# How the queries are turned in a transformer block on one core: an fp32r product with a cast identity, or an fp32 transposition

## The chip, the cores and the metric

The kernel runs on one core of a Trainium2 chip. The metric is the device time of one execution in microseconds; the median of 3 runs before the change is 634.89 us (634.57 to 635.85).

## The reference

16 sequences of 512 tokens with 256 features pass through an attention block and a linear layer with quantised inputs, each with a layer norm ahead and behind and a residual sum. The attention has 16 heads of 16 features and replaces the exponential by its second-order expansion. What is normalised is the sum of 1 + s + s²/2 over the queries (the kernel can therefore sum products of features over the whole sequence once, instead of forming all 512 x 512 scores).

```python
def _taylor_softmax(x):
    t = 1.0 + x + 0.5 * x * x
    return t / jnp.sum(t, axis=-1, keepdims=True)
h = (x - mu) * jax.lax.rsqrt(var + EPS) * ln_w + ln_b
q = h @ w_q
kv = h @ w_kv
k, v = (kv[..., :DIMS], kv[..., DIMS:])
q, k, v = (to_heads(q), to_heads(k), to_heads(v))
q = _rope(q, theta)
k = _rope(k, theta)
qk = jnp.einsum('bhkd,bhqd->bhkq', q, k) * scale
attn = _taylor_softmax(qk)
wv = jnp.einsum('bhkq,bhqd->bhkd', attn, v)
wv = wv.transpose(0, 2, 1, 3).reshape(B, T, DIMS)
return wv @ w_o
...
x = x + _layernorm(_L0_attn_ref(_layernorm(x, axis=-1), L0_attn_ln_w, L0_attn_ln_b, L0_attn_w_q, L0_attn_w_kv, L0_attn_w_o, L0_attn_theta), axis=-1)
x = x + _layernorm(_L0_ffn_ref(_layernorm(x, axis=-1), L0_ffn_weight, L0_ffn_bias), axis=-1)
```

The linear layer rounds its inputs and its weights in blocks of 32 to a grid of 6-bit values and multiplies them (`xd @ wd.T + bias`).

## The kernel before, in words

The tokens are cut into 64 tiles of 128 (4 to a sequence). Every tile goes through the same stages, and the stages of several tiles are interleaved. The order in which each engine issues its stages is written out in a table: `ORDER` gives, for each engine and stage, the step at which each tile's turn comes, and the function `step` of the engine calls in each step the stages whose turn it is. Engines wait for one another by semaphores only.

The stages of a tile, with the engine on which they run:

- the tile is normalised (VectorE) and turned by TensorE (`turn_z`, L894, two transpositions of 128 x 128); ScalarE copies the upper part (`high_h`, L1241), VectorE the rest (L1613)
- keys and queries (`project_kq`) and values (`project_v`) are products in which the high and the low part of each operand are multiplied in turn (`split_product`, L783, L784, L786)
- VectorE rotates keys and queries; ScalarE rounds the queries to fp32r and writes them as the high part into `qsp` (`high_q`, L1293), and GpSimd the difference as the low part (`low_q`, L1764)
- `turn_q` (L883): TensorE turns `qsp` in four blocks of 128 x 128 into the PSUM bank `ps_tr`, and ScalarE copies the bank to `qT` as fp32r (`copy_q`, L1261)
- products of the key features are summed over the sequence (`sum_features`, L1032, on 32 columns of the array each); once a sequence the sums are turned (`turn_sums`, L1041) and combined (`rest_matrix`, L1050, L1057)
- `select` (L859, five a tile, 512 columns each) sums pairs of query features; ScalarE squares the result (`square`, L1192, L1194); `attend` (L924, L930, on 32 columns each) multiplies by the summed keys
- the attended values go out and in by DMA, are normalised, multiplied by the output weights (`project_out`), rounded, turned (`turn_ffn_input`, L873) and multiplied (`ffn`). In the last two sequences the attended values are turned on the core instead (`turn_quads`, L962, four transpositions, and `turn_attention`, L952).

The bank `ps_tr` is shared by `turn_z`, `turn_q`, `turn_ffn_input` and `project_v`; `turn_bank_is_free` waits for the copies of all that were issued before. A turned block is the product of the block as the array's weights and the identity as what streams through, or a transposition with the same operands. The identity comes by DMA into `small` (`ident`) and is used as it is by all transpositions. For `turn_q` ScalarE casts it once, at the start, to `identr` in fp32r (`cast_identity`, L1102), ahead of the scaled identities of `turn_weights` (L1108 to L1111), for which the first products of the weights wait (`fold_kq`, L796, L799). Before those products TensorE runs 12 pairs of fp32 products of ones (`warm_up`, L825), and two of them at some places of the first steps (`fill`, L825).

Of the kernel before, what the change touches and what calls it, by code (L numbers as in the profile page):

```python
# [7 lines left out]
ACT = mybir.ActivationFunctionType  # L8
AX = mybir.AxisListType
F32 = mybir.dt.float32  # L10
F32R = mybir.dt.float32r
FP8 = mybir.dt.float8e4

P = 128
# [88 lines left out]
        "warm_up": ((0,), (), ()),  # L103
    }),
    "scalar": (71, {
        "cast_identity": ((0,), (), ()),
        "cast_selection": ((2,), (), ()),
        "centre": ((133, 150, 167, 175, 195, 220, 238, 254, 274, 291, 310, 325, 345, 363, 381, 396, 412, 432, 452, 467,
            486, 501, 520, 538, 558, 574, 592, 609, 629, 646, 665, 682, 700, 717, 736, 754, 771, 785, 807, 823, 842,
# [220 lines left out]
            150, 151, 152, 153, 154, 155, 156, 157, 158, 159, 160, 161,)),  # L330
    }),
}
RATE = {"angles": "once", "bias_mean": "once", "cast_identity": "once", "cast_selection": "once", "centre_bias": "once",
    "constant": "sequence", "copy_ffn_weight": "once", "copy_main": "sequence", "copy_rest": "sequence", "copy_sums":
    "sequence", "ffn_weight_mean": "once", "fold_kq": "once", "fold_v": "once", "frequencies": "once", "high_kq":
    "once", "high_v": "once", "invert_denominators": "tail", "invert_sums": "spread", "load_again": "load",
# [11 lines left out]
def places(table, count):  # L348

    first, cycle, last, pitch = table  # L350
    steps = {}
    for index in range(count):
        if index < len(first):
            place = first[index]
        elif index >= count - len(last):
            place = last[index - count + len(last)]
        else:
            place = cycle[index % len(cycle)] + pitch * (index // len(cycle))
        steps[place] = index
    return steps  # L360
# [56 lines left out]
def sandwich(nc, x, w_q, w_kv, w_o, weight, bias, identity, columns, selection, out):  # L417
# [7 lines left out]
    for engine, (pitch, tables) in ORDER.items():  # L425
        for name, table in tables.items():
            plan[name] = places(table + (pitch,), counts[RATE.get(name, "tile")])
            issued[name] = 0
# [10 lines left out]
    def each(n, name, stage, *args):  # L439

        if n in plan[name]:
            stage(Tile(plan[name][n]), *args)
            issued[name] += 1

    def once(n, name, stage):

        if n in plan[name]:
            index = plan[name][n]
            stage(Tile(NT * index + NT - 1))
# [21 lines left out]
    def setup(n, name, stage):  # L471

        if n in plan[name]:
            stage()
# [17 lines left out]
    with ExitStack() as ctx:  # L492
        def sb(name, shape, dt=F32):
            return ctx.enter_context(nc.sbuf_tensor(name, shape, dt))

        def bank(name):
            return ctx.enter_context(nc.psum_tensor(name, [P, 512], F32))

        def sem(name):
            return ctx.enter_context(nc.semaphore(name))  # L500


        ps_tr = bank("ps_tr")
# [8 lines left out]
        ident = small[:, 0:P]  # L512
# [2 lines left out]
        pos = small[:, P + 2:P + 2 + NT]  # L515
        freq_base = small[:, P + 6:P + 14]
        cmat = small[0:NP, P + 32:P + 32 + 2 * HD]
        identr = sb("identr", [P, P], F32R)
        selr = sb("selr", [P, CHUNKS, P], F32R)
        at = P + 32 + 2 * HD  # L520
        th = small[:, at:at + 1]
# [27 lines left out]
        qsp = sb("qsp", [P, 2, NQ, 2, HQ * HD], F32R)  # L549
# [75 lines left out]
        const_in, sel_cast, cols_in, ident_in = sem("const_in"), sem("sel_cast"), sem("cols_in"), sem("ident_in")  # L625
        x0_in, table_chain, angles_done, sines_done, tables_done, ln_scaled = (
            sem("x0_in"), sem("table_chain"), sem("angles_done"), sem("sines_done"), sem("tables_done"), sem("ln_scaled"))
        corner_done, turn_ready, kq_folded, v_folded = sem("corner_done"), sem("turn_ready"), sem("kq_folded"), sem("v_folded")
        wkq_in, wv_in, ffn_in, identr_cast, wo_in = sem("wkq_in"), sem("wv_in"), sem("ffn_in"), sem("identr_cast"), sem("wo_in")
        setup_chain, setup_pool, wd_ready, wdt_done = sem("setup_chain"), sem("setup_pool"), sem("wd_ready"), sem("wdt_done")  # L630
        wdt_copied, floor_set, wdt_centred, wo_centred = sem("wdt_copied"), sem("floor_set"), sem("wdt_centred"), sem("wo_centred")
        wkq_high, wkq_low, wv_high, wv_low, wdt_high, wdt_low, wo_high, wo_low = (
# [144 lines left out]
        def _(pe):  # L777
# [84 lines left out]
            def turn_bank_is_free():  # L862

                wait(pe, hT_low, issued["turn_z"])
                wait(pe, qT_copied, issued["turn_q"])
                wait(pe, xdT_low, issued["turn_ffn_input"])
                wait(pe, v_copied, issued["project_v"])
# [6 lines left out]
                mm.then_inc(xdT_done, 1)  # L874

            def turn_q(t):
                if t.n == 1:
                    pe.wait_ge(identr_cast, 1)
                pe.wait_ge(qlo_ready, t.n)
                turn_bank_is_free()  # L880
                for qd in range(NQ):

                    mm = pe.matmul(ps_tr[:, qd * P:(qd + 1) * P], qsp[:, t.two, qd].rearrange("p a b -> p (a b)"), identr[:, :],  # L883
                                   start=True, stop=True)
                mm.then_inc(qT_done, 1)

            def turn_z(t):
# [174 lines left out]
            def step(n):  # L1062
                idle(n, "fill", fill)
                idle(n, "drain", drain)
                setup(n, "warm_up", warm_up)
                setup(n, "fold_kq", fold_kq)
                setup(n, "fold_v", fold_v)
                each(n, "sum_features", sum_features)
                each(n, "select_2", select, 2)
                each(n, "project_v", project_v)  # L1070
                each(n, "select_3", select, 3)
                each(n, "ffn", ffn)
                each(n, "select_4", select, 4)
                each(n, "turn_q", turn_q)
                once(n, "turn_sums", turn_sums)
                tail(n, "turn_quads", turn_quads)
                each(n, "project_kq", project_kq)
                each(n, "turn_z", turn_z)
                each(n, "select_0", select, 0)
                setup(n, "turn_ffn_weight", turn_ffn_weight)  # L1080
                each(n, "project_out", project_out)
                each(n, "select_1", select, 1)
                each(n, "turn_ffn_input", turn_ffn_input)
                once(n, "rest_matrix", rest_matrix)
                tail(n, "turn_attention", turn_attention)
                each(n, "attend", attend)
# [5 lines left out]
        def _(act):  # L1092
# [3 lines left out]
            act.dma_start(wkqv[:, :, 2 * D:3 * D], kv[:, :, D:2 * D]).then_inc(wv_in, 16)  # L1096
            act.wait_ge(setup_pool, 16)
            act.activation(warm[:], mhalf[:], ACT.Sin)

            def cast_identity():  # L1100
                act.wait_ge(ident_in, 16)
                act.activation(identr[:], ident, ACT.Copy).then_inc(identr_cast, 1)  # L1102

            def turn_weights():

# [223 lines left out]
            def step(n):  # L1329
                setup(n, "turn_weights", turn_weights)  # L1330
                setup(n, "high_v", high_v)
                setup(n, "high_kq", high_kq)
                each(n, "high_q", high_q)
                each(n, "square_4", square, 4)
                each(n, "copy_q", copy_q)
                setup(n, "split_ffn_weight", split_ffn_weight)
                each(n, "square_k", square_k)
                setup(n, "weight_distance_sizes", weight_distance_sizes)
                setup(n, "copy_ffn_weight", copy_ffn_weight)
                each(n, "centre", centre)  # L1340
                once(n, "copy_main", copy_main)
                setup(n, "weight_low", weight_low)
                setup(n, "sum_wo", sum_wo)
                each(n, "square_s", square_s)
                each(n, "square_y", square_y)
                each(n, "high_ffn_input", high_ffn_input)
                setup(n, "centre_bias", centre_bias)
                each(n, "high_h", high_h)
                setup(n, "weight_size", weight_size)
                setup(n, "sum_bias", sum_bias)  # L1350
                each(n, "high_attention", high_attention)
                once(n, "copy_rest", copy_rest)
                each(n, "square_0", square, 0)
                setup(n, "weight_high", weight_high)
                each(n, "square_f", square_f)
                each(n, "square_1", square, 1)
                each(n, "copy_quad", copy_quad)
                once(n, "copy_sums", copy_sums)
                each(n, "square_2", square, 2)
                each(n, "copy_v", copy_v)  # L1360
                setup(n, "cast_identity", cast_identity)
                setup(n, "cast_selection", cast_selection)
                setup(n, "split_wo", split_wo)
                setup(n, "sines", sines)
                each(n, "square_3", square, 3)

            every_step("scalar", step)


# [487 lines left out]
```

## Time and profile before

| | |
|---|---|
| median of 3 runs | 634.89 us |
| the profiled execution | 634.73 us |
| its span, first to last instruction | 632.9 us |
| mean granted TensorE clock | 0.992 |
| TensorE (PE) busy | 607.2 us |
| VectorE (DVE) busy | 579.3 us |
| ScalarE (ACT) busy | 534.0 us |
| GpSimd (POOL) busy | 393.8 us |

All times are microseconds from the first instruction of one profiled execution. Matmuls overlap: the next begins before the last has ended, so that busy times and durations of single matmuls cannot be added; starts can be compared. A row of the timeline that ends in x4 is four instructions of one line, and its second number runs from the first start to the last end. PEld is the load of the weights into the array, which may run ahead while an earlier matmul streams. An L number is a line of the kernel.

### The profile page before, as it was taken

To read this page: it belongs to the slowest core of one execution; us is meant where nothing else is said; L and a number is where in the kernel's file an instruction comes from. 1 tells how busy PE (TensorE), PEld (TensorE's weight loads), DVE (VectorE), ACT (ScalarE), POOL (GpSimd) and SP (SyncE) were. 2 spreads that over 40 slices of the span, in tenths; PEclk is the share of its full clock that TensorE was granted. 3 is DMA by queue.
4 is the path that set the end of the run, shared out by engine and by line. 5 is a ranking of instruction groups with operands and counts; after the bars stand their busy time and mean duration, and the time that the engine had idled before them with its cause. 6 is when DMAs were issued, how large, how long until landed. Compare 5 with 4: busy or idle time off the path is not lost.

```text
span 632.9 us, 22530 instructions
## 1 busy us (share of the span) xinstructions
PE 607.2 (96%) x7588; PEld 470.3 (74%) x7588; DVE 579.3 (92%) x1425; ACT 534.0 (84%) x1505; POOL 393.8 (62%) x597
## 2 busy tenths in 40 slices
PE   8799999999999999999999999999999999999984
PEld 8677667777777787777777777777778777778763
DVE  5999999999999999999999999999999999987796
ACT  4357769898898989989899889899898888899983
POOL 2575366676666567766766777675765767653343
PEclk9999999999999999999999999999999999999996
DMA  7101131222232232223232231323233222230201
GB/s 251 35 3 39 24 76 23 66 77 74 60 95 63 76 91 64 76 49 93 73 105 62 79 83 42 108 55 97 62 83 84 68 49 52 69 85 20 68 27 51
DMA packets 55951, 43.64 MB, mean 69 GB/s; under 512 B 7200, under 2 KB 55712, under 8 KB 55840
## 3 DMA queue, kind: packets, MB, share of 16 engines
q1 hardware_dynamic: 55024, 41.42, 24.6%
q8 instruction: 64, 1.05, 0.7%
q10 hardware_dynamic: 816, 0.79, 0.4%
q14 instruction: 47, 0.39, 0.2%
HBM read 18.65 MB, written 8.39 MB: 43 GB/s over the span
## 4 chain that ended last, share of the span: by engine, by line
PE 87%; ACT 5%; issue 4%; DVE 3%; POOL 1%; POOLq 0%; ACTq 0%; DVEq 0%
PE ps_f L859 12%; PE ps_mt L1032 12%; PE ps_o L930 5%; PE ps_o L924 5%; PE ps_qk L783 5%; PE ps_qk L784 5%; PE ps_qk L786 5%; PE ps_w L783 4%; PE ps_tr L883 4%; PE ps_f L924 4%; PE ps_w L786 4%; PE ps_w L784 4%; PE ps_tr L783 3%; PE ps_tr L873 3%; PE ps_tr L786 2%
## 5 line engine op out<-in xcount | busy, mean ns | idle before, releaser
L1192 ACT ACTIVATE feat<-ps_f 128x512 f32<-128x512 f32 x256 | 147.5, 600 | 13.0 <-PE ps_f L859 12.4
L678 DVE TENSOR_TENSOR kf<-kf 128x672 f32<-128x672 f32 (+1 forms) x128 | 130.4, 1023 | 1.0
L859 PE MATMUL ps_f<-qT,selr 128*128 128x512 f32 x320 | 120.4, 426 | 2.0 <-ACT feat L1192 1.2
L1032 PE MATMUL ps_mt<-kf,vp 128*32 128x153 f32 x2048 | 79.6, 296 | 1.5 <-DVE kf L678 0.5
L1787 POOL TENSOR_TENSOR rs_f<-var_f,mhalf 128x1 f32<-128x1 f32 x64 | 47.9, 749 | 47.5 <-ACT squares_f L1326 46.5
L1787 POOL TENSOR_TENSOR rs_y<-var_y,mhalf 128x1 f32<-128x1 f32 x64 | 47.3, 740 | 41.9 <-ACT squares_y L1304 41.4
L1032 PEld LDWEIGHTS ps_mt<-kf,vp 128*32 128x32 f32 x2048 | 60.3, 109 | 16.7 <-issue 14.5
L1776 POOL TENSOR_TENSOR kf<-kf 128x128 f32<-128x128 f32 x64 | 36.6, 571 | 47.2 <-DVE kf L1543 47.2
L859 PEld LDWEIGHTS ps_f<-qT,selr 128*128 128x128 f32 x320 | 55.2, 188 | 13.3 <-ACT feat L1192 5.4
L1783 POOL TENSOR_TENSOR attT_l<-att,attT_h 128x256 fp32r<-128x256 f32 x56 | 45.0, 805 | 31.1 <-ACT attT_h L1233 31.0
L678 POOL TENSOR_TENSOR kf<-kf 128x224 f32<-128x224 f32 x64 | 58.2, 909 | 3.9 <-DVE kf L1548 3.8
L1764 POOL TENSOR_TENSOR qsp<-kf,qsp 128x256 fp32r<-128x256 f32 x64 | 54.2, 847 | 5.9 <-ACT qsp L1293 5.7
L1787 POOL TENSOR_TENSOR rs_s<-var_s,mhalf 128x1 f32<-128x1 f32 x64 | 43.2, 674 | 20.8 <-ACT squares_s L1319 20.3
L783 PE MATMUL ps_qk<-wkqv_h,hT_l 128*128 128x512 f32 x128 | 54.1, 422 | 0.0
L784 PE MATMUL ps_qk<-wkqv_l,hT_h 128*128 128x512 f32 x128 | 50.7, 396 | 0.0
L1261 ACT ACTIVATE qT<-ps_tr 128x512 fp32r<-128x512 f32 x64 | 38.5, 601 | 10.8 <-PE ps_tr L883 9.7
L1787 POOL TENSOR_TENSOR rs_x<-vx,mhalf 128x1 f32<-128x1 f32 x64 | 43.3, 677 | 4.0
L1194 ACT ACTIVATE feat<-ps_f,small 128x512 f32<-128x512 f32 x64 | 44.3, 693 | 1.6 <-PE ps_f L859 1.4
L924 PE MATMUL ps_o<-feat,main 120*32 120x256 f32 (+1 forms) x576 | 42.0, 361 | 2.4 <-ACT feat L1192 2.0
L1529 DVE TENSOR_TENSOR kf<-ps_qk,cosT 128x512 f32<-128x512 f32 x64 | 43.2, 676 | 1.0 <-PE ps_qk L786 0.6
L930 PE MATMUL ps_f<-feat,rm 64*32 64x256 f32 (+1 forms) x576 | 42.0, 363 | 0.0
L930 PE MATMUL ps_o<-feat,rm 64*32 64x256 f32 (+1 forms) x576 | 42.0, 363 | 0.0
(205 smaller groups left out, 1900.3 us busy)
## 6 DMA issues: line engine op xcount, KB each, us to landing
xc<-L_attn_x SPq DMA_DIRECT2D x16, 512.0 KB, 4.0
result<-fin SPq DMA_DIRECT2D x64, 128.0 KB, 1.9
xa<-L_attn_x SPq DMA_DIRECT2D x15, 512.0 KB, 4.0
heads_out<-osb SPq DMA_DIRECT2D x224, 32.0 KB, 2.0
shares<-sums SPq DMA_DIRECT2D x112, 64.0 KB
sums<-osb SPq DMA_DIRECT2D x224, 2.0 KB
wkqv<-L_attn_w_kv ACTq DMA_DIRECT2D x2, 256.0 KB, 4.6
xa<-L_attn_x SPq DMA_DIRECT2D x1, 384.0 KB, 6.1
```

Source lines behind the costliest of these rows:

```text
L678: return eng.tensor_tensor(dims(row, F_MAIN, [[FW, heads], [HD, NR - 1], [1, HD]]), dims(row, F_LIN, [[FW, heads], [0, NR - 1], [1, HD]]), ...
L783: pe.matmul(out_, xl(c), wh(c), start=c == 0, stop=False)
L784: pe.matmul(out_, xh(c), wl(c), start=False, stop=False)
L786: mm = pe.matmul(out_, xh(c), wh(c), start=False, stop=c == CH - 1)
L859: pe.matmul(ps_f[i % 2][:, :], selr[:, i], queries, start=True, stop=True).then_inc(sel_done, 1)
L924: pe.matmul(attend_bank(e)[VW * j:VW * (j + 1), part(p)], main[0:NP, par, p + 2 * e, VW * j:VW * (j + 1)], feat[0:NP, p2, 2 * e + j % 2, t ...
L930: mm = pe.matmul(attend_bank(e)[VW * j:VW * (j + 1), part(p)], rm[rows, par, p, j], feat[rows, p2, HQ, tokens(p, j)], start=False, stop=Tr ...
L1032: mm = pe.matmul(ps_mt[qd // 2][VW * h:VW * (h + 1), (qd % 2) * NF:(qd % 2 + 1) * NF], vp[:, s2, qd * HQ + h], kf[:, s2, qd * HQ + h, 0:NF ...
L1192: act.activation(feat[:, p2, i], ps_f[i % 2][:, :], ACT.Square).then_inc(squared, 1)
L1764: pool.tensor_tensor(dims(qsp[:, p2], HQ * HD, [[2 * HQ * HD, NQ], [HD, HQ], [1, HD]]), dims(kf[:, p2, 0, 0:1], F_Q, [[HQ * FW, NQ], [FW, ...
L1783: pool.tensor_tensor(attT_l[:, t.two].rearrange("p c n -> p (c n)"), att[:, t.two], attT_h[:, t.two].rearrange("p c n -> p (c n)").bitcast ...
L1787: pool.tensor_tensor(rs[c][:, t.two:t.two + 1], variance[:, t.two:t.two + 1], mhalf[:], ALU.pow).then_inc(rstd[c], 1)
```

## The change

`turn_q` turns the four blocks by a transposition in fp32, with the plain identity, in place of a product in fp32r with the cast identity. The cast, its buffer of 512 bytes a partition and its semaphore go. The lines behind the places where something went move up by some lines.

```diff
-        "cast_identity": ((0,), (), ()),
...
-        identr = sb("identr", [P, P], F32R)
...
             def turn_q(t):
-                if t.n == 1:
-                    pe.wait_ge(identr_cast, 1)
                 pe.wait_ge(qlo_ready, t.n)
                 turn_bank_is_free()
                 for qd in range(NQ):
 
-                    mm = pe.matmul(ps_tr[:, qd * P:(qd + 1) * P], qsp[:, t.two, qd].rearrange("p a b -> p (a b)"), identr[:, :],
-                                   start=True, stop=True)
+                    mm = pe.transpose(ps_tr[:, qd * P:(qd + 1) * P], qsp[:, t.two, qd].rearrange("p a b -> p (a b)").bitcast(F32), ident)
                 mm.then_inc(qT_done, 1)
...
-            def cast_identity():
-                act.wait_ge(ident_in, 16)
-                act.activation(identr[:], ident, ACT.Copy).then_inc(identr_cast, 1)
```

Apart from the cast no instruction goes, comes or moves. On ScalarE the start of its order of instructions was this (warm is a one-column activation that loads the table, wa and wb hold the scaled identities):

```order
4 L1098 ACT_TABLE_LOAD
5 L1098 ACTIVATE warm<-mhalf 128x1
6 L1102 ACTIVATE identr<-small 128x128
7 L1108 ACTIVATE wa<-small,lnwx 128x128
8 L1109 ACTIVATE wa<-small,lnwn 128x128
9 L1111 ACTIVATE wa<-wb,lnwx 128x127
```

and is now this:

```order
4 L1093 ACT_TABLE_LOAD
5 L1093 ACTIVATE warm<-mhalf 128x1
6 L1099 ACTIVATE wa<-small,lnwx 128x128
7 L1100 ACTIVATE wa<-small,lnwn 128x128
8 L1102 ACTIVATE wa<-wb,lnwx 128x127
```

The cast has gone, and what stood behind it moved up by one place. On TensorE this is one place of the body before (a turned tile of queries, L883, between the end of a split product and two selects):

```order
748 L786 MATMUL ps_w<-wdt_h,xdT_h 128x256 x2
749 L883 MATMUL ps_tr<-identr,qsp 128x128 x4
750 L859 MATMUL ps_f<-qT,selr 128x512 x2
751 L1041 MATMUL ps_mt<-small,mts 120x128 x4
752 L894 MATMUL ps_tr<-small,z 128x128 x2
753 L783 MATMUL ps_w<-wo_h,attT_l 128x256
```

and now:

```order
748 L784 MATMUL ps_w<-wdt_h,xdT_h 128x256 x2
749 L879 MATMUL ps_tr<-small,qsp 128x128 x4
750 L857 MATMUL ps_f<-qT,selr 128x512 x2
751 L1036 MATMUL ps_mt<-small,mts 120x128 x4
752 L889 MATMUL ps_tr<-small,z 128x128 x2
753 L781 MATMUL ps_w<-wo_h,attT_l 128x256
```

Nothing moved; the four blocks read `small`, which holds the plain identity, in place of `identr`.

## Rows read from the trace of the kernel before

**Rows 1.** The page: busy shares, clock in tenths by slice, chain by engine.
```profile
PE 607.2 (96%) x7588; PEld 470.3 (74%) x7588; DVE 579.3 (92%) x1425; ACT 534.0 (84%) x1505; POOL 393.8 (62%) x597
...
PEclk9999999999999999999999999999999999999996
...
PE 87%; ACT 5%; issue 4%; DVE 3%; POOL 1%; POOLq 0%; ACTq 0%; DVEq 0%
```

**Rows 2.** Stretches: length, busy us of PE, PEld, DVE, ACT, POOL; clock, DMA, GB/s.
```profile
20.00:40.00 20.00, 18.38 (x190) 15.59 (x189) 19.46 (x40) 7.13 (x19) 12.50 (x17) 1.00 0.10 29
200.00:300.00 100.00, 99.61 (x1277) 77.47 (x1279) 95.58 (x236) 90.69 (x258) 67.40 (x99) 1.00 0.28 71
616.00:633.00 17.00, 7.77 (x43) 6.16 (x41) 11.18 (x32) 6.46 (x25) 6.06 (x10) 0.71 0.14 47
```

**Rows 3.** Groups by line: busy us, mean ns of one, idle before.
```profile
L883 PE MATMUL ps_tr<-identr,qsp 128*128 128x128 f32 x256 | 37.3, 268 | 1.4 <-POOL qsp L1764 1.0
...
L962 PE MATMUL ps_mt<-small,osb 128*128 128x128 f32 x32 | 4.7, 274 | 0.0
...
L883 PEld LDWEIGHTS ps_tr<-identr,qsp 128*128 128x128 f32 x256 | 35.6, 190 | 7.9 <-issue 5.2
...
L962 PEld LDWEIGHTS ps_mt<-small,osb 128*128 128x128 f32 x32 | 3.6, 140 | 0.4 <-issue 0.4
```

**Rows 4.** Timeline of PE, products loaded ahead: start, us, line, operation.
```profile
378.01 0.56 PE L883 MATMUL ps_tr<-identr,qsp 128*128 128x128 f32 x4
378.41 0.68 PE L859 MATMUL ps_f<-qT,selr 128*128 128x512 f32 x2
378.93 0.28 PE L783 MATMUL ps_w<-wo_h,attT_l 128*128 128x256 f32 x1
```

**Rows 5.** Timeline of PE, transpositions loaded ahead, the same neighbours.
```profile
597.27 0.60 PE L962 MATMUL ps_mt<-small,osb 128*128 128x128 f32 x4
597.63 0.72 PE L859 MATMUL ps_f<-qT,selr 128*128 128x512 f32 x2
598.18 0.28 PE L783 MATMUL ps_w<-wo_h,attT_l 128*128 128x256 f32 x1
```

**Rows 6.** Timeline of PE, products not loaded ahead.
```profile
341.39 0.63 PE L883 MATMUL ps_tr<-identr,qsp 128*128 128x128 f32 x4
...
342.38 0.28 PE L783 MATMUL ps_w<-wo_h,attT_l 128*128 128x256 f32 x1
```

**Rows 7.** Timeline of PE, transpositions not loaded ahead.
```profile
593.67 0.63 PE L962 MATMUL ps_mt<-small,osb 128*128 128x128 f32 x4
594.05 0.48 PE L859 MATMUL ps_f<-qT,selr 128*128 128x512 f32 x1
594.37 0.38 PE L873 MATMUL ps_tr<-small,xd 128*128 128x128 f32 x2
```

**Rows 8.** Timeline of PE, products before narrow matmuls.
```profile
314.35 0.56 PE L883 MATMUL ps_tr<-identr,qsp 128*128 128x128 f32 x4
314.83 0.60 PE L1032 MATMUL ps_mt<-kf,vp 128*32 128x153 f32 x12
```

**Rows 9.** Timeline of PE, two transpositions before narrow matmuls.
```profile
173.21 0.38 PE L894 MATMUL ps_tr<-small,z 128*128 128x128 f32 x2
173.51 0.58 PE L1032 MATMUL ps_mt<-kf,vp 128*32 128x153 f32 x9
```

**Rows 10.** Timeline of the start: the cast, and the first product of the weights.
```profile
5.60 0.31 ACT L1102 ACTIVATE identr<-small 128x128 fp32r<-128x128 f32 x1 [1.84 <-DMA small<-identity]
...
10.86 1.03 PE L796 MATMUL ps_f<-wkqv,wa 128*128 128x256 f32 x4
```

**Rows 11.** Waits: who for whom, us in total, times, longest.
```profile
ACT qT L1261 <- PE ps_tr L883: 9.7, 18, 1.7
```

**Rows 12.** Timeline of PE, a pair of fp32 products of ones.
```profile
17.54 0.61 PE L825 MATMUL ps_o<-one 128*128 128x128 f32 x4
```

More of the change, by code:

```diff
@@ L332 @@
 }
-RATE = {"angles": "once", "bias_mean": "once", "cast_identity": "once", "cast_selection": "once", "centre_bias": "once",
+RATE = {"angles": "once", "bias_mean": "once", "cast_selection": "once", "centre_bias": "once",
     "constant": "sequence", "copy_ffn_weight": "once", "copy_main": "sequence", "copy_rest": "sequence", "copy_sums":
@@ L628, in sandwich @@
         corner_done, turn_ready, kq_folded, v_folded = sem("corner_done"), sem("turn_ready"), sem("kq_folded"), sem("v_folded")
-        wkq_in, wv_in, ffn_in, identr_cast, wo_in = sem("wkq_in"), sem("wv_in"), sem("ffn_in"), sem("identr_cast"), sem("wo_in")
+        wkq_in, wv_in, ffn_in, wo_in = sem("wkq_in"), sem("wv_in"), sem("ffn_in"), sem("wo_in")
         setup_chain, setup_pool, wd_ready, wdt_done = sem("setup_chain"), sem("setup_pool"), sem("wd_ready"), sem("wdt_done")
@@ L1360, in step @@
                 each(n, "copy_v", copy_v)
-                setup(n, "cast_identity", cast_identity)
                 setup(n, "cast_selection", cast_selection)
```

## The prediction

> **What bounds the kernel now.** I read the page first: the busy shares, the slices, the shares of the chain that ended last. TensorE (PE) is busy 96% of the span and holds 87% of the chain; its granted clock is full in every slice but the last [rows 1]. Then the stretches: from 200 to 300 us PE is busy 99.61 of 100 us, VectorE 95.58, ScalarE 90.69 [rows 2]. So PE's order of work sets the pace of the body. VectorE has only 4 us in 100 to spare, so a gain on PE need not come through whole. A busy share does not price a matmul, because neighbouring ones overlap: one of 128 columns is shown with 268 ns [rows 3], yet four of them in a row take 0.56 us, not 1.07. The price is therefore read from start to start: when the group starts and when the instruction behind it can start, taken far enough behind it that the pace is regular again.
>
> **The change part by part.** 64 times (once a tile) PE turns four 128 x 128 blocks of queries. Before, each is a product in fp32r with a cast identity (L883, 256 in all); after, a transposition in fp32 with the plain identity. Nothing is moved. The same operation on the same shape stands in this trace: the four transpositions of L962 in the tail, and pairs at L873 and L894. So no price has to be guessed; only the surroundings differ.
>
> The two are slow in different places. The weight load of an fp32r block takes 190 ns, that of a transposition 140 [rows 3]. The row of four products is 0.56 us from first start to last end, and the next matmul starts 0.40 us after the first [rows 4]; the row of four transpositions is 0.60 us, with the next 0.36 us after the first [rows 5]. One matmul of either takes about 0.27 us to its end (268 and 274 ns, rows 3), so the transpositions start (0.60 - 0.27) / 3 = 0.11 us apart. Four kinds of place come out of this.
>
> 1. Weights loaded ahead, a full-width matmul behind (either a select, L859, or a split product). Products: from the group's start, over two selects, to the L783 behind them, 378.93 - 378.01 = 0.92 us [rows 4]. Transpositions with the very same neighbours: 598.18 - 597.27 = 0.91 us [rows 5]. The transpositions let the next matmul start earlier, but that one then holds the engine longer. Gain 0.01 us.
>
> 2. Weights not loaded ahead (the group's first load had to wait), full-width matmul behind. Products: 342.38 - 341.39 = 0.99 us over two selects [rows 6]. Transpositions: 594.37 - 593.67 = 0.70 us over one select [rows 7]; a second one adds 0.23 us, since two selects hold the engine 598.18 - 597.63 = 0.55 us behind transpositions [rows 5] and one holds it 594.37 - 594.05 = 0.32 us [rows 7]; so 0.93. Gain 0.06 us.
>
> 3. Weights loaded ahead, narrow matmuls behind, each on 32 columns of the array (L1032, L924, L1050). Products: 314.83 - 314.35 = 0.48 us until the first narrow one starts [rows 8]. Transpositions: a pair takes 173.51 - 173.21 = 0.30 us [rows 9], two more add 0.22, so 0.52. Loss 0.04 us.
>
> 4. Other transpositions or fill products behind, and the cold places before narrow matmuls: nothing, within 0.02 us each.
>
> How many of each? A group loaded ahead lasts 0.56 us [rows 4] and one that is not 0.63 [rows 6]; the whole line is 37.3 us [rows 3]. From 0.56 n + 0.63 (64 - n) = 37.3 follows n = 43 loaded ahead and 21 not. Going through PE's order of instructions, 9 of the 64 are followed by narrow matmuls, 5 by transpositions or fill, 50 by full-width ones; seven of the nine are of the kind loaded ahead. I take 34 places of the first kind, 17 of the second, 7 of the third, 6 of the fourth.
>
> Sum on PE: -34 x 0.01 - 17 x 0.06 + 7 x 0.04 = -0.34 - 1.02 + 0.28 = -1.1 us.
>
> The cast of the identity (L1102, 0.31 us on ScalarE at 5.60 us) goes, and the scaled identities behind it move up by about that [rows 10]. Their first reader, L796, starts at 10.86 us, after the warm-up products; the cast is covered by some 4 us, so I count nothing. Without that cover it would be 0.3 us. SBUF loses a tile of 512 bytes a partition and everything behind it moves; no row prices that, I take nothing.
>
> A second effect has the other sign. ScalarE copies the turned queries (L1261), and it waits for L883 18 times, 9.7 us in total [rows 11]. In the 43 places loaded ahead the last of four ends at 0.60 instead of 0.56 us. Where ScalarE already waits, that is at most 18 x 0.04 = 0.7 us later. ScalarE has 5% of the chain [rows 1], so nearly all of this lies beside PE's other work; I put down 0.04 us and keep the 0.7 for the range.
>
> Not all of PE's 1.1 us arrives. 17 of the places that gain are those at which PE waited for the split of the queries, and a group that comes up sooner there waits longer. I take the middle of nothing and all weighted by the chain's PE share, about two thirds: -0.7 us. The profiled execution took 634.73 us (span 632.9 and 1.8 around it), so 634.0; it lies 0.16 below the median 634.89, on whose footing this is 634.2 us. A difference under 0.2%, 1.3 us, is what a measurement of this kernel can hardly tell from none.
>
> A rule that speaks against the change: the granted clock is 1.00 from 200 to 300 us with four transpositions a tile already in it, and fell to a mean of 0.71 only after 616 us, where PE is busy 7.77 of 17 us [rows 2]; the transposed groups raise the transpositions from four to eight a tile. The Trainium skill ("TensorE: Matmul & The Clock Gate", Part 4) says that a transposition does not count as activity the way a product does. By that rule eight a tile could let the clock fall; the trace so far shows no sign of it. The sum would stay -0.7 us without it; with it, it is the third rival.
>
> **The rivals.**
>
> Faster than forecast: the gain of kind 2 holds nearly everywhere, because what I called loaded ahead is in the changed kernel limited by loads, and those get shorter. PE's weight loads shrink by 256 x 50 ns = 12.8 us [rows 3]. Price 55 x 0.06 = 3.3 us less 0.3 for the narrow neighbours: 3.0, so 631.9. For it: the fp32r loads, 190 ns, are what spaces the products. Against it: the pair of rows 4 and 5 with equal neighbours shows 0.01.
>
> Slower: the later end decides. The copy of the queries starts 0.04 us later at each of 43 places; it holds up ScalarE's queue (square, copy_v and so on stand behind it, in order), those free PE's banks, and PE waits. Price 43 x 0.04 = 1.7 us, with none of the gain coming through and the narrow places losing 0.3: 636.9. It decides once ScalarE rather than PE is waited for in most tiles; it is at 90.69 of 100 us. Against it: the chain has ScalarE at 5%.
>
> Slower by the clock: in 20 to 40 us, while the pipeline fills, PE is busy 18.38 of 20 us, less densely than later, and there the first turned tiles pass [rows 2]. If the clock fell from its upper to its lower level (2.4 to 1.2 GHz) for 8 us of work, that work would take up to 8 us more. VectorE, busy 19.46 of 20 us there, hides a part; price 3 to 6 us, 639.
>
> That it does not do what it says: the blocks go through as true fp32 products. The fill products of L825 are such; two of them are four records of which each starts about (0.61 - 0.27) / 3 = 0.11 us after the last [rows 12], 0.22 a product. 256 x (0.22 - 0.11) = 28 us more, 662. The existing transpositions each leave one record, so I hold it for very unlikely.
>
> **How the numbers follow.** Forecast 634.2 us, chance 0.68; its own range is 633.0 to 635.8 (all of PE's gain and half as much again; none of it and the whole 0.7 of the copies, plus the spread of the median). Faster rival 0.14; slower by the copies 0.14; by the clock 0.03; not as it says 0.01. The range for 8 in 10 reaches into both near rivals: 632.4 to 636.8. Faster by over 0.2%, below 633.6: 0.08 of the forecast's 0.68 and the 0.14, so 0.22. Slower, above 636.2: 0.02 of the forecast and 0.18, so 0.20. Within: 0.58.
>
> **What would show it.** In the profile after: the four of the query line spaced 0.11 us, a group 0.60 us loaded ahead and 0.63 not, the line's busy sum 64 x 0.6 = 39 us instead of 37.3; their loads 140 ns, PE's load row lower by about 13 us; the matmul behind starting 0.36 us after the group's start; 0.91 us over two selects. ScalarE without the cast and the same start of L796. A clock under 1.00 in any stretch before 616 us would mean the clock rival; more waiting of ScalarE for the turned queries, and of PE for the squares, the copy rival; two records a block the last. The forecast is wrong if the span moves by over 1.3 us with all of these as said: then the waits between engines, not PE's own pace, carried the change.

## The result: no gain, slower by 0.27% in one comparison and not to be told from before in two

In the first comparison (20 runs of each) the changed kernel took 636.13 us in the median, the one before 634.19: ratio 1.0027, 95% interval 1.0017 to 1.0036. The forecast was 634.2 and a gain of 0.7 us; the direction is wrong. Two more comparisons of the same kernel (12 runs against 35 each) gave 0.9999 (0.9981 to 1.0016) and 1.0002 (0.9990 to 1.0015), and the kernel before against itself gave 0.9989 (0.9974 to 1.0005). The first interval overlaps neither of the two others of the changed kernel, so there is a part that the intervals do not cover. What the changed kernel costs lies by the three ratios between 0 and 0.3%; the gain of 0.7 us that was forecast shows in none of them.

The profiled execution after has a span of 634.3 us (before: 632.9). The page, answering to [rows 1]:

```profile
PE 607.2 (96%) x7588; PEld 465.4 (73%) x7588; DVE 580.3 (91%) x1425; ACT 533.4 (84%) x1504; POOL 393.8 (62%) x597
...
PEclk9999999999999999999999999999999999999997
...
PE 87%; ACT 5%; issue 4%; DVE 3%; POOL 1%; POOLq 0%; ACTq 0%; DVEq 0%
```

PE's sum is the same to the tenth, ScalarE has one instruction fewer, the shares of the chain are unchanged, and the clock row reads 9 in every slice but the last (by stretches it is 1.00 up to 616 us). From 200 to 300 us (columns as in rows 2):

```profile
200.00:300.00 100.00, 99.65 (x1281) 76.67 (x1284) 95.49 (x236) 90.38 (x259) 67.58 (x99) 1.00 0.27 71
```

The groups by line, answering to [rows 3] (L879 is the old L883):

```profile
L879 PE MATMUL ps_tr<-small,qsp 128*128 128x128 f32 x256 | 39.0, 275 | 1.2 <-issue 0.9
...
L879 PEld LDWEIGHTS ps_tr<-small,qsp 128*128 128x128 f32 x256 | 29.6, 140 | 8.9 <-issue 5.3
```

39.0 us and 140 ns are the forecast values; a transposition leaves one record, so it is one. The row of the loads is lower by 6.0 us (35.6 to 29.6), the sum of PEld by 4.9, where 12.8 was forecast: 256 x 50 ns counts loads that overlap in the row twice (256 x 190 ns would be 48.6 us, the row has 35.6). The timeline of PE at a group loaded ahead, answering to [rows 4]:

```profile
378.84 0.60 PE L879 MATMUL ps_tr<-small,qsp 128*128 128x128 f32 x4
379.21 0.70 PE L857 MATMUL ps_f<-qT,selr 128*128 128x512 f32 x2
379.75 0.28 PE L781 MATMUL ps_w<-wo_h,attT_l 128*128 128x256 f32 x1
```

From the group to L781 it is 0.91 us (before 0.92). The same for a group not loaded ahead [rows 6], and for one before narrow matmuls [rows 8]:

```profile
342.26 0.63 PE L879 MATMUL ps_tr<-small,qsp 128*128 128x128 f32 x4
...
343.19 0.28 PE L781 MATMUL ps_w<-wo_h,attT_l 128*128 128x256 f32 x1
```

```profile
314.08 0.60 PE L879 MATMUL ps_tr<-small,qsp 128*128 128x128 f32 x4
314.61 0.86 PE L1027 MATMUL ps_mt<-kf,vp 128*32 128x153 f32 x20
```

0.93 us against 0.99, and 0.53 against 0.48: each local price came out as read off beforehand, to 0.01 us. What takes the gain back is elsewhere.

### Where the time went, by the starts of the same instructions

PE runs the same 7588 matmuls in the same order in both kernels. So the start of each can be subtracted from the start of the same one in the first profile of before, and the growth of this difference cut into pieces: up to the first turned tile; the groups (from the matmul ahead of one to the third behind it), apart for the 19 tiles whose weights are not loaded ahead (1, 5, 8, 11, 13, 15, 16, 24, 29, 38, 40, 50, 52, 54, 55, 56, 57, 60, 63) and the 45 others; the stretches between groups, with those under 0.15 us summed and the larger ones (steps) listed with the tile they follow; and what is behind the last group. In us, minus is earlier than before; the kernels are those of the experiments below.

| kernel | start | 19 groups | 45 groups | small pieces | steps (tile) | behind |
|---|---|---|---|---|---|---|
| before again (e9) | -0.44 | 0.01 | 0.01 | 0.03 | 0.20 (16) | -0.57 |
| changed | -0.91 | -0.90 | 0.17 | 0.80 | 0.19 (1), 0.42 (21), 1.12 (37), 1.07 (61) | -0.56 |
| changed (e1) | -0.32 | -0.93 | 0.19 | 0.84 | 0.18 (1), 0.42 (21), 0.18 (34), -0.30 (35), 0.96 (37), 1.07 (61) | 0.01 |
| changed (e5) | -0.02 | -0.93 | 0.08 | 0.71 | 0.18 (1), 0.39 (21), 0.44 (27), 0.22 (61) | -0.56 |
| padded (e6) | -0.55 | -0.94 | 0.09 | 0.59 | 0.18 (1), 0.40 (21), 0.35 (27), 0.15 (37), 0.20 (38), 0.24 (61), 0.34 (62) | -0.35 |
| cast kept (e2) | -0.31 | -0.83 | 0.13 | 0.76 | 0.41 (21), 0.32 (37) | -1.12 |
| all but tile 21 (e7) | -0.79 | -0.81 | 0.90 | 0.59 | 1.98 (37) | -0.03 |
| the 45 only (e4) | -0.37 | -0.09 | 0.12 | 0.41 | 0.39 (21), 0.19 (23), 0.17 (55), 0.35 (62) | -0.17 |
| tile 21 only (e8) | -0.35 | -0.07 | 0.18 | -0.30 | 0.40 (21), 0.17 (55), 0.66 (61) | -1.10 |
| the 19 only (e3) | -0.72 | -0.81 | 0.15 | 0.13 | 0.20 (16) | -0.57 |
| the 19 only (e10) | -0.44 | -0.72 | 0.87 | 0.09 | 0.41 (62) | -0.60 |

(In e7 and e10 steps fell into groups of the 45: 0.58 us at tile 37 in e7, 0.50 at tile 22 and 0.30 at tile 46 in e10.) Four things stand out. The start and the end differ by up to 0.9 us between profiles of one and the same kernel, so they are no part of the change (both follow the clock, see below). The 19 groups give 0.7 to 0.9 us, always when they are transpositions. The small pieces are 0.6 to 0.8 us in every kernel with the transposition in all or all but one of the tiles, 0.41 with it in the 45, and between -0.30 and 0.13 in the four profiles in which the 45 (or all but tile 21) are products; the column is good to some 0.3 us, no better. And the step of 0.4 us behind tile 21 is there in every kernel in which tile 21 is transposed, and in no other.

**The small pieces: a wait for the copy.** Summed by the pair of matmuls around them over 50 to 560 us, they stand mostly before or behind the turned z (L894) and before selects and narrow matmuls that wait: between a select and turn_z 0.3 to 0.4 us, between turn_z and a select 0.4, in each profile of the changed kernel. At nine turned z between 200 and 433 us turn_z starts 0.20 or 0.21 us after the end of the copy of the queries, in before and in all three profiles of the changed kernel; these nine give 0.44 us. At 13 others the select behind turn_z starts 0.53 to 0.55 us after the copy's end, where it had been 0.55 to 0.58; these give 0.41. At the nine, then, the copy sets the start in both kernels, and at the 13 in the changed one. One of the nine, first in the profile of before: the group of tile 23, ScalarE's copy of it, and the next user of the bank.

```profile
207.59 0.56 PE L883 MATMUL ps_tr<-identr,qsp 128*128 128x128 f32 x4
...
208.18 0.61 ACT L1261 ACTIVATE qT<-ps_tr 128x512 fp32r<-128x512 f32 x1
...
209.00 0.41 PE L894 MATMUL ps_tr<-small,z 128*128 128x128 f32 x2
```

The same in the profile after:

```profile
207.14 0.60 PE L879 MATMUL ps_tr<-small,qsp 128*128 128x128 f32 x4
...
207.78 0.60 ACT L1252 ACTIVATE qT<-ps_tr 128x512 fp32r<-128x512 f32 x1
...
208.58 0.41 PE L889 MATMUL ps_tr<-small,z 128*128 128x128 f32 x2
```

The copy begins 0.59 us after the group's start before and 0.64 after, because the last of four blocks ends at 0.60 instead of 0.56; turn_z, which needs the bank, follows at 1.41 and 1.44. PE, which had saved nothing here, loses 0.03 us. ScalarE waits for the queries 20 times, 10.1 us (18 times, 9.7 us in rows 11):

```profile
ACT qT L1252 <- PE ps_tr L879: 10.1, 20, 1.5
```

**The step behind tile 21: 0.05 us decide which of two engines goes first.** Before, VectorE and GpSimd around 193 us:

```profile
193.30 1.08 DVE L678 TENSOR_TENSOR kf<-kf 128x896 f32<-128x896 f32 x1
193.32 1.47 POOL L1787 TENSOR_TENSOR rs_f<-var_f,mhalf 128x1 f32<-128x1 f32 x1
...
194.69 0.41 DVE L1512 TENSOR_SCALAR z<-xa,mv,rs_x 128x255 f32<-128x255 f32 x1
194.76 0.54 POOL L1787 TENSOR_TENSOR rs_y<-var_y,mhalf 128x1 f32<-128x1 f32 x1
```

And after:

```profile
192.40 0.55 POOL L1777 TENSOR_TENSOR rs_f<-var_f,mhalf 128x1 f32<-128x1 f32 x1
192.43 1.10 DVE L676 TENSOR_TENSOR kf<-kf 128x896 f32<-128x896 f32 x1
...
193.85 0.94 DVE L1502 TENSOR_SCALAR z<-xa,mv,rs_x 128x255 f32<-128x255 f32 x1
193.91 0.74 POOL L1754 TENSOR_TENSOR qsp<-kf,qsp 128x256 fp32r<-128x256 f32 x1
```

Tile 21 is one of the groups before narrow matmuls. Behind it PE, then ScalarE's copy of the turned z and VectorE's hT_l, come 0.05 us later against GpSimd. Before, VectorE's kf starts 0.02 us ahead of GpSimd's rs_f, and rs_f takes 1.47 us. After, rs_f is ahead by 0.03 us and takes 0.55. GpSimd has thereby come further when VectorE reaches z: z now runs beside the long qsp and takes 0.94 us instead of 0.41. VectorE's chain is near enough to PE's that 0.4 us of the 0.53 arrive at PE. The same two orders stand in all twelve profiles: rs_f takes 1.47 or 1.48 us and z 0.40 or 0.41 in the five with products in tile 21, 0.54 or 0.55 and 0.94 in the seven with transpositions there.

**The large steps: waits that come and go.** The step behind tile 37 is VectorE waiting for the DMA of the sums. Before, after, and in the third profile of the changed kernel, in this order:

```profile
334.80 0.94 DVE L1582 RECIPROCAL sums<-sums 64x128 f32<-64x128 f32 x1
```

```profile
335.61 0.94 DVE L1572 RECIPROCAL sums<-sums 64x128 f32<-64x128 f32 x1 [0.95 <-DMA sums<-osb]
```

```profile
335.62 0.94 DVE L1572 RECIPROCAL sums<-sums 64x128 f32<-64x128 f32 x1
```

The changed kernel waits 0.95 us in one execution and nothing in another, at the same place. SyncE issues the DMAs of four heads one behind another (some 2.3 us for four, as x4 rows of its timeline show), and in the first profile after the issues began 1.1 us later than before, at 329.95 against 328.88. In the third they began as late, at 329.86, but there PE's work was 1.06 us later than in the first, and nothing was left to wait for; behind the place both profiles are 0.87 us behind the one before. So this wait takes back what an earlier start had gained. Behind tile 61 there is, in the first profile after, a gap on PE in the middle of a run of matmuls for which nothing is waited:

```profile
555.11 0.27 PE L925 MATMUL ps_f<-feat,rm 64*32 64x128 f32 x1
555.82 0.27 PE L925 MATMUL ps_o<-feat,rm 64*32 64x128 f32 x1 [0.45 <-issue]
```

In that profile a fetch of instructions (DMA queue 8) had ended at 554.45 us. The step is 1.07 us in two profiles of the changed kernel and 0.22 in the third. The gap goes with the fetch: it stands in three of the twelve profiles (changed, e1, e8), and in these the matmul behind it starts 1.37, 1.30 and 1.35 us after the end of the last fetch; in the nine others the same matmul starts 2.15 us or more after it, and there is no gap. e8 has products in all tiles but one and its buffers laid out as before, so the gap belongs neither to the transposition nor to the layout. That a late fetch makes it is read from these profiles; no experiment moved a fetch.

**The start and the end: the clock.** The columns for the start and the end follow the moments at which the granted clock rises and falls. It is first on record, as full, at 8.66 us before and at 6.72, 8.00 and 8.62 in the three profiles of the changed kernel; the start column there is -0.91, -0.32 and -0.02. At the end it falls to the lower level at 623.1 us before, with 9.9 us to go (e1: 9.4, column 0.01), in five profiles with 6.3 to 7.0 us to go (columns -0.56 to -0.60), in e2 and e8 with 3.7 and 3.2 (-1.12 and -1.10). The same stretch before and in e8, columns as in rows 2:

```profile
624.00:626.00 2.00, 1.97 (x8) 1.57 (x8) 1.74 (x4) 0.00 (x0) 0.53 (x1) 0.50 0.00 0
```

```profile
624.00:626.00 2.00, 1.31 (x8) 0.97 (x8) 1.87 (x7) 0.57 (x3) 1.31 (x2) 1.00 0.19 66
```

This also spreads the times. In the three later comparisons the kernel before averages 635.5 us over its 18 executions with a mean granted clock of 0.992, and 633.4 over the 14 with 0.997.

An estimate that takes it out (a straight line in the mean clock through the 208 executions of these comparisons, with a constant for each comparison and each kernel) has the changed kernel 0.45 us slower than before (95%: give or take 0.4), the one with the cast kept 0.64 and the padded one 0.65 (0.6 each), the transposition in the 45 tiles alone 1.04 slower (0.6), in the 19 alone 0.60 faster (0.4), and e7 and e8 within 0.2 of before (0.6). That is the order and about the size of the pieces. The first comparison has no clocks on record for before and is not in it.

### The profile page after: what moved, and what is told of

It is laid out like the page before. It is cut to its first block, busy times and chain, and to the rows that moved or that the text cites. A ratio compares the mean times of both kernels' runs of the same rounds, so it can differ in the third digit from the quotient of the medians.

```text
span 634.3 us, 22528 instructions
## 1 busy us (share of the span) xinstructions
PE 607.2 (96%) x7588; PEld 465.4 (73%) x7588; DVE 580.3 (91%) x1425; ACT 533.4 (84%) x1504; POOL 393.8 (62%) x597
## 4 chain that ended last, share of the span: by engine, by line
PE 87%; ACT 5%; issue 4%; DVE 3%; POOL 1%; POOLq 0%; ACTq 0%; DVEq 0%
PE ps_mt L1027 12%; PE ps_f L857 11%; PE ps_o L925 5%; PE ps_o L919 5%; PE ps_qk L781 5%; PE ps_qk L782 5%; PE ps_qk L784 5%; PE ps_tr L879 5%; PE ps_w L781 4%; PE ps_f L919 4%; PE ps_w L784 4%; PE ps_w L782 4%; PE ps_tr L781 3%; PE ps_tr L871 3%; PE ps_tr L889 2%
## 5 line engine op out<-in xcount | busy, mean ns | idle before, releaser
L857 PE MATMUL ps_f<-qT,selr 128*128 128x512 f32 x320 | 121.7, 429 | 2.0 <-ACT feat L1183 1.2
L781 PE MATMUL ps_qk<-wkqv_h,hT_l 128*128 128x512 f32 x128 | 54.2, 423 | 0.0
L1252 ACT ACTIVATE qT<-ps_tr 128x512 fp32r<-128x512 f32 x64 | 38.5, 601 | 12.0 <-PE ps_tr L879 10.1
```

What stands on the lines that cost most here:

```text
L781: pe.matmul(out_, xl(c), wh(c), start=c == 0, stop=False)
L857: pe.matmul(ps_f[i % 2][:, :], selr[:, i], queries, start=True, stop=True).then_inc(sel_done, 1)
```

## The experiments

### e1, e5: the changed kernel again

No edit.

> The changed kernel once more, for a second profile and for the ratio on this chip. Every theory expects 1.7 to 2.0 us slower than before in the times (636.1 against 634.2 in the comparison that is known). Theory A (what PE gains locally, 0.7 us over the 64 groups, is given back and more at waits, since the last of four blocks ends 0.04 us later in the 45 groups loaded ahead): the stretches between the groups are longer in sum by 1 us or more, in many small pieces of 0.03 to 0.08 us, also in this profile. Theory B (a few stalls of about 1 us, as at 340 us and 554 us of the first profile after, make the difference and belong to the changed kernel): they come again at the same places. Theory C (those stalls are chance): they are at other places or missing.

Ratio 0.9999 (0.9981 to 1.0016); the common expectation of 1.7 us failed. In the profile the small pieces are there (0.84 us, as theory A says), and the two large steps at the same places (as theory B says).

> The changed kernel a third time, for the ratio and a third profile. The two comparisons so far gave 1.0027 (1.0017 to 1.0036) and 0.9999 (0.9981 to 1.0016). Theory A (what PE gains at the groups is given back at waits, with a small loss left): between 1.000 and 1.003. Theory B (stalls that belong to the changed kernel): the VectorE wait for the DMA of the sums near 335 us (0.3 us or more longer than before), the PE stall of 0.7 us near 555 us right behind an instruction fetch, and the 0.53 us longer z operation near 194.7 us are all three there again. Theory C (chance): at least one of them is missing.

Ratio 1.0002 (0.9990 to 1.0015). The step behind tile 37 is missing and that behind tile 61 is 0.22 instead of 1.07: theory C holds for these two. z takes 0.94 us and the step behind tile 21 is there for the third time. Without these two, and without other steps that do not come again, the changed kernel's own pieces (19 groups, 45 groups, small pieces, steps behind 1 and 21) sum to 0.68, 0.70 and 0.43 us in the three profiles.

### e2, e6: the operation, the cast, the layout

e2, against before:

```diff
-                    mm = pe.matmul(ps_tr[:, qd * P:(qd + 1) * P], qsp[:, t.two, qd].rearrange("p a b -> p (a b)"), identr[:, :],
-                                   start=True, stop=True)
+                    mm = pe.transpose(ps_tr[:, qd * P:(qd + 1) * P], qsp[:, t.two, qd].rearrange("p a b -> p (a b)").bitcast(F32), ident)
```

> The queries turned by the fp32 transposition as in the changed kernel, but the cast of the identity, its buffer and its semaphore are kept as before, so that every tile of SBUF lies where it did and ScalarE's start is unchanged. If the operation itself is the cause (theory A), the time is that of the changed kernel, 1.7 us above before (ratio 1.0027). If the shift of the tiles in SBUF or the missing cast is the cause (theory D), it is within 0.3 us of before.

Ratio 1.0005 (0.9991 to 1.0019): too wide to choose by time. The profile does: small pieces 0.76 us and 0.41 behind tile 21 as in the changed kernel. They belong to the operation. Only the 0.18 us behind tile 1 is missing; it is in all four profiles without the cast and in none with it, so the missing cast goes with that much while the pipeline fills. It lies at two places where narrow matmuls (sum_features) follow the fill products, 0.11 us near 32 us and 0.05 to 0.07 near 36; why they start later there was not followed.

e6, against the changed kernel:

```diff
+        spare = sb("spare", [P, P])
         selr = sb("selr", [P, CHUNKS, P], F32R)
```

> The changed kernel with an unused buffer of 512 bytes a partition where the cast identity lay, so that SBUF is laid out as before; the cast itself stays away. The 0.7 us PE stall near 555 us was in both profiles of the changed kernel and not in the one with the cast kept. If the layout makes it, it is gone here; if the missing cast (one instruction fewer on ScalarE, one wait fewer on PE) or the instruction stream makes it, it is there. In time: at most 0.7 us below the changed kernel in the first case.

Ratio 0.9998 (0.9984 to 1.0012). The stall is not there (0.24 us behind tile 61), but e5, the changed kernel with its own layout, lacks it too (0.22), and e8, laid out as before, has it; so this says nothing of the layout. The small pieces and tile 21 are there. Nothing speaks for an effect of where the tiles lie.

### e3, e10, e4: one kind of group at a time

```diff
+UNLOADED = (1, 5, 8, 11, 13, 15, 16, 24, 29, 38, 40, 50, 52, 54, 55, 56, 57, 60, 63)
...
+                    if t.n in UNLOADED:
+                        mm = pe.transpose(...)
+                    else:
+                        mm = pe.matmul(...)
```

(e4 has `not in`.)

> The transposition only in the 19 tiles whose group's first weight load had to wait (1, 5, 8, 11, 13, 15, 16, 24, 29, 38, 40, 50, 52, 54, 55, 56, 57, 60, 63), the fp32r products in the other 45; cast kept. Theory A: there the transposition starts the next matmul 0.06 us earlier and ends no later, so 0 to 1.1 us faster than before, and nothing lost. Theory B/D: no difference from before, or slower by a share of 19/64 (0.5 us).

Ratio 0.9977 (0.9964 to 0.9990). The 19 groups give 0.81 us, the small pieces are 0.13, tile 21 makes no step: 0.5 us gained in the profile. The ratio promises more than that.

> Transpositions in the 19 tiles whose weights were not loaded ahead, products in the other 45, once more (the first time 0.9977, 0.9964 to 0.9990). Theory A: 0.8 us gained at the groups, 0.1 to 0.3 given back: ratio 0.998 to 0.9995, below 1. If the first was chance: 1.000 and above half the time.

Ratio 0.9988 (0.9971 to 1.0005), beside 0.9989 for the kernel before itself in the same comparison; medians 633.87 and 634.17. In the body the gain shows again (0.72 at the groups, 0.09 given back), in the time it can't be told from none. It is the best of the variants, by some 0.5 us of its first profile. That it beats before is shown by the times of e3 and not by those of its repeat; with the clock taken out as above both together are 0.6 us faster (0.2 to 1.0), an estimate made after the fact.

> The opposite: the transposition in the 45 tiles whose weights were loaded ahead, products in the 19 others; cast kept. Theory A: all of the loss and none of the gain, 1.7 to 2.8 us slower than before. A theory by which each transposition costs the same: 45/64 of the loss, 1.2 us. Theory D: no difference from before.

Ratio 1.0006 (0.9991 to 1.0022): theory A had 1.7 to 2.8 us slower, and even the upper end of the interval is 1.4. The profile has its pieces: nothing gained at the groups (-0.09 and +0.12), 0.41 small pieces, 0.39 behind tile 21.

### e7, e8: tile 21 alone

The condition is `t.n != 21` in e7 and `t.n == 21` in e8, otherwise as above.

> Transpositions in all tiles but tile 21 (its group is followed by narrow matmuls, and PE is 0.04 to 0.06 us later behind it than with products), cast kept. Theory A': those 0.05 us change the order in which VectorE and GpSimd come to run side by side at 194.7 us: z takes 0.94 us instead of 0.41, and the rest of the kernel runs 0.4 us later. Then here z takes 0.41 us and the step of +0.4 us at 198 us is missing, everything else as with the cast kept. If the step comes from something else in the chain (earlier groups), it is there.

> The reverse: products in all tiles but tile 21. Theory A': one group of four transpositions suffices: z at 194.7 us takes 0.94 us and the step of 0.4 us is there, the only difference from before in the body. If it needs the shifts of several groups: z takes 0.41 us and there is no step. In time 0 to 0.4 us slower than before.

At z and behind tile 21 both are as theory A' says. Products in tile 21 alone (e7):

```profile
192.28 1.08 DVE L678 TENSOR_TENSOR kf<-kf 128x896 f32<-128x896 f32 x1
192.29 1.48 POOL L1790 TENSOR_TENSOR rs_f<-var_f,mhalf 128x1 f32<-128x1 f32 x1
...
193.68 0.41 DVE L1515 TENSOR_SCALAR z<-xa,mv,rs_x 128x255 f32<-128x255 f32 x1
```

Transpositions in tile 21 alone (e8):

```profile
192.80 0.55 POOL L1790 TENSOR_TENSOR rs_f<-var_f,mhalf 128x1 f32<-128x1 f32 x1
192.84 1.10 DVE L678 TENSOR_TENSOR kf<-kf 128x896 f32<-128x896 f32 x1
...
194.25 0.94 DVE L1515 TENSOR_SCALAR z<-xa,mv,rs_x 128x255 f32<-128x255 f32 x1
```

In e7 the order is that of before and there is no step; in e8, where only the four matmuls of one tile differ from before, the order is the other one, and PE is 0.40 us later behind it. Not all of this stays: at 327 us e8 is 0.24 us later against its own start, and the profile with the cast kept (e2) 0.31 more than e7. That nothing else would differ did not hold for either: e7 has the step behind tile 37, e8 the gap behind tile 61 (0.66) and small pieces of -0.30. The times do not resolve it: e7 0.9998 (0.9986 to 1.0010), with the longest wait of VectorE for the sums of all profiles (1.82 us), e8 0.9994 (0.9981 to 1.0007).

### e9: the kernel before against itself

No edit.

> The kernel before itself, against itself: shows what a ratio of no change looks like on a chip here, and gives a second profile of it. Ratio 1.000, interval within 0.9985 to 1.0015. In the profile z at 194.7 us takes 0.41 us again (theory A': the order of VectorE and GpSimd there hangs on PE's timing behind tile 21); if the chance stalls (VectorE waiting for the DMA of the sums near 335 us, PE near 550 us) belong to no kernel, at least one step of over 0.15 us against the first profile is found somewhere.

Ratio 0.9989 (0.9974 to 1.0005). z takes 0.41 us, small pieces 0.03 us, one step of 0.20 us. The starts differ by 0.44 us, those of the end by 0.57. As expected z takes 0.41 us and there is a step; the interval is wider than the expected 0.9985 to 1.0015 and lies lower.

### e11, e12: the group twice

```diff
-                for qd in range(NQ):
+                for qd in [q for again in range(2) for q in range(NQ)]:
```

> The four products of each tile issued twice in a row (the same blocks into the same places, 256 more in all). Each adds 0.111 us on PE: 28.4 us if PE's time passes whole, 20 if VectorE and ScalarE hide a third of it. The turned block ends 0.44 us later in each tile: by the rival that the later end decides (0.04 us cost 1.7 us), it would cost much more than PE's 28 us.

> The four transpositions of each tile issued twice in a row, cast kept. Each adds 0.109 us on PE: 27.9 us against the kernel with them once, so within 1 us of the products twice. If a transposition had a price that the starts do not show, this one is clearly the slower of the two.

Medians 659.31 and 659.82 against 634.46: 24.9 and 25.4 us for 256 blocks, 0.097 and 0.099 us each. Of PE's 28.4 and 27.9 us, 87% and 91% arrive. So the two operations have the same price inside a row, and most of PE's added time passes. They do not decide on the copy rival: a turned block that ends 0.44 us later in each tile would by that rival cost 64 x 0.44 = 28.2 us, the same as PE's own time, and the two delays run side by side and do not add up. PE's groups by line, e11 and then e12:

```profile
L883 PE MATMUL ps_tr<-identr,qsp 128*128 128x128 f32 x512 | 65.8, 271 | 1.3 <-POOL qsp L1764 1.0
```

```profile
L883 PE MATMUL ps_tr<-small,qsp 128*128 128x128 f32 x512 | 67.0, 274 | 1.3 <-POOL qsp L1763 1.0
```

## Why the prediction was wrong, step by step

- **What bounds the kernel**: right. PE's extra time passes to about 0.9 (e11, e12), more than the two thirds that were put down for a gain; no run takes 28 us away, so for a gain the share is not shown.
- **The local prices, kinds 1 to 3**: right to 0.01 us, and the count of groups not loaded ahead was 19 instead of 21. Their gain is 0.90 to 0.93 us in the three profiles of the changed kernel where 1.02 was forecast; the other 45 cost 0.08 to 0.19 where -0.06 was.
- **The cast**: covered at its place, as said: L796's successor L794 starts right behind the warm-up, at 9.94 us instead of 10.86 [rows 10], but that is the warm-up, of which each profile has another length (the start column: -0.02 to -0.91 for the same changed kernel). That without it the kernel would be 0.18 us later behind tile 1 was not forecast.
- **The copies**: the step that failed. "I put down 0.04 us and keep the 0.7 for the range" has it the wrong way round: the pieces given back at waits are 0.7 to 0.8 us in the three profiles of the changed kernel and 0.03 in the repeat of before. With the third of PE's gain that was not to arrive, the sum gave back 0.4 us in all; the runs gave back about all that the groups had gained. ScalarE's 5% of the chain was read as the weight of a delay of 0.04 us. But a wait of a few hundredths shows in no share: between overlapping matmuls it is no idle time.
- **Collisions of VectorE and GpSimd**: no term at all. A shift of 0.05 us made a step of 0.4 us (shown by e7 and e8 from both sides), of which 0.24 to 0.31 was left at 327 us.
- **The sum**: -0.9 + 0.15 + 0.75 + 0.4 + 0.18 = +0.6 us from the pieces that came again in every profile, 0.1%, in place of -0.7. The three profiles have 0.43 to 0.70. The rest of the first comparison's 1.9 us is not assigned: its cause stays open. The waits for the DMA of the sums and the stall behind tile 61 are larger in the all-transposed kernels (sum of the steps other than behind 1 and 21: 2.19, 1.91, 0.66, 1.28, 0.32 and 1.98 us) than in the others (0.20, 0.71, 0.83, 0.20 and 0.41), but they vary from 0.66 to 2.19 within one kernel. Whether a slightly later SyncE makes them likelier stays open. The prediction's last sign (a span that moves by over 1.3 us with all local signs as said) came, 632.9 to 634.3; but one kernel's own spans lie from 633.4 to 635.2, so a single pair of profiles could not have shown it.
- **The rivals**: the slower one by the copies had the right mechanism, at some 20 places and not 43 and at 0.02 to 0.06 us each; that no gain at all comes through is contradicted by the 0.9 us of the 19 groups, of which e3 and e10 give back 0.1. The faster one is out: groups loaded ahead do not gain. The granted clock stayed 1.00 before 616 us, with eight transpositions a tile; the Trainium skill's rule ("TensorE: Matmul & The Clock Gate", Part 4) had no visible effect here. The change does what it says.
- **The range**, 632.4 to 636.8, held the median of the first comparison, 636.13; the sign did not hold. That the two later medians, 634.58 and 635.02, lie within 0.9 us of the forecast 634.2 is no merit of the sum: two of its terms were wrong.

## What to carry to other kernels

Price an operation from start to start and by what stands ahead of and behind it: here the same swap gains 0.06 us where the weight load had to wait, nothing where it ran ahead, and loses 0.05 us before narrow matmuls. Where several engines run at over 90% in a hand-set order, set the default for such a gain of tenths of a microsecond to "given back at the next shared buffer", and look which neighbour engine runs beside which in the original, because an order fitted to the old times can lose more by a shift of 0.05 us than the operation gains. And compare two or more profiles of each kernel before a step between two of them is explained: of the four largest steps of the first pair, two were small or gone in the changed kernel's third profile. Where the time of a kernel follows its granted clock, set executions of like mean clock side by side: here 2 us hang on it, more than the change is worth.

## What the runs showed of the hardware

- When VectorE's 896-column product starts 0.02 us ahead of a one-column operation of GpSimd, the latter takes 1.47 us; when it starts 0.03 us behind, 0.55 us, and VectorE's own takes 1.10 instead of 1.08. Beside GpSimd's 256-column subtraction a 255-column operation of VectorE takes 0.94 us instead of 0.41.
- A row of fp32 transpositions 128 x 128 and a row of fp32r products of the same size have the same price inside the row, 0.099 and 0.097 us in the time of the kernel, though the weight loads take 140 and 190 ns.
- The time until the first products of the weights differs by up to 0.9 us between executions of the same kernel, since the 24 warm-up products take longer or shorter:

```profile
2.46 7.64 PE L823 MATMUL ps_o<-one 128*128 128x128 f32 x48 [2.46 <-POOL rm L1723]
```

  In this profile they start 0.21 us apart until 6.7 us and 0.11 us from then on; the granted clock is on record from 6.72 us on, as 1.00 (2.4 GHz), and that the lower level (1.2 GHz) stands ahead of it is read from the doubled distance alone. In the profile of before the change came at 8.7 us (on record from 8.66), and the row was 8.57 us long.
- Near 555 us a gap of 0.4 to 0.7 us on PE, for which nothing is waited, stands in the three profiles in which a fetch of instructions (16 KB) had ended only 1.30 to 1.37 us before the matmul behind the gap, and in none of the nine in which it had ended 2.15 us or more before.
